# The head of a three-block kernel: first transposes tile by tile, low parts ahead of the next statistics, recursion steps apart

## The reference

```
x = x + 0.5 * ffn(layernorm(x))
x = x + ssm(layernorm(x))
x = x + 0.5 * ffn(layernorm(x))

def ffn(x):                                   # tokens x 256
    shared = silu(x @ sg.T) * (x @ su.T) @ sd.T
    logits = x @ gate_w.T                     # 8 experts
    top_id, score = argmax(logits), sigmoid(max(logits))
    routed = sum over e of swiglu_e(where(top_id == e, x * score, 0))
    return shared + routed

def ssm(x):
    u = conv4(x @ W_in + b_in) + conv_b       # 512 channels, depthwise, causal
    h = tanh(A) h + u * Bp ;  y = Cp . h + Dp * u      # 16 states, step by step
    return silu(y) @ W_out + b_out
```

## Time and profile before

| | us |
|---|---|
| median of 3 executions | 859.96 |
| lowest, highest | 859.24, 860.71 |
| the profiled execution | 860.55 |
| its span in the trace | 858.5 |
| PE busy | 827.7 (96%) |
| DVE, ACT, POOL busy | 485.3, 391.5, 461.1 |

### The profile page before, as it was taken

How to read it: one execution, slowest core, us unless ns; L and a number is a source line. 1 busy time by engine, 2 the same in 40 slices (tenths; PEclk the granted TensorE clock), 3 DMA queues, 4 the chain that set the end, 5 groups by cost and what they waited for, 6 DMA issues and landing times.

```text
span 858.5 us, 16219 instructions
## 1 busy us (share of the span) xinstructions
PE 827.7 (96%) x5302; PEld 720.7 (84%) x5303; DVE 485.3 (57%) x983; ACT 391.5 (46%) x766; POOL 461.1 (54%) x444
## 2 busy tenths in 40 slices
PE   4999999999999999999999999999999999999896
PEld 3678988888888888888888888888888888888786
DVE  7888753333333336678999886867333333333364
ACT  4743323334334434556777787233243434434331
POOL 6528870333333058859999992687330333330584
PEclk9999999999999999998999999999999999999999
DMA  9963553645464337310010015155345564431366
GB/s 309 327 260 105 177 167 118 208 159 215 157 229 163 104 62 144 48 26 13 7 56 26 26 51 197 50 166 192 127 134 198 189 213 174 157 123 43 94 157 179
DMA packets 52005, 119.07 MB, mean 139 GB/s; under 512 B 6442, under 2 KB 39860, under 8 KB 47604
## 3 DMA queue, kind: packets, MB, share of 16 engines
q0 software_dynamic: 16624, 75.25, 27.7%
q1 hardware_dynamic: 34834, 43.15, 15.4%
q10 hardware_dynamic: 498, 0.02, 0.0%
HBM read 83.25 MB, written 35.14 MB: 138 GB/s over the span
## 4 chain that ended last, share of the span: by engine, by line
PE 72%; POOL 14%; DMA 6%; issue 4%; DVE 3%; ACT 1%; POOLq 0%; DVEq 0%; SPq 0%; ACTq 0%
PE bank L424 21%; PE bank L426 21%; PE bank L425 20%; POOL xs_sorted L1868 4%; PE bank L631 4%; POOL yr L2062 3%; PE bank L600 2%; DMA wr_hi<-w_routed 2%; DMA xT_kept<-xTf_odd 2%; POOL acc L1942 2%; POOL wr_lo L1912 2%; DVE v L1554 1%; PE bank L491 1%; POOL wr_lo L1904 1%; PE bank L502 1%
## 5 line engine op out<-in xcount | busy, mean ns | idle before, releaser
L1912 POOL TENSOR_TENSOR wr_lo<-wr_raw,wr_hi 128x3072 fp32r<-128x3072 f32 x14 | 95.5, 6819 | 94.7 <-DMA wr_hi<-w_routed 86.4
L424 PE MATMUL bank<-wr_hi,xT_hi 128*128 x312 | 130.2, 417 | 1.1 <-POOL wr_lo L1912 1.1
L1209 DVE TENSOR_TENSOR hT_lo<-bank,hT_hi 128x512 fp32r<-128x512 f32 x78 | 54.0, 692 | 124.6 <-ACT hT_hi L884 124.6
L1512 DVE TENSOR_TENSOR hf<-sg,bank 128x512 f32<-128x512 f32 x78 | 53.7, 688 | 124.3 <-PE bank L426 124.3
L426 PE MATMUL bank<-wr_lo,xT_hi 128*128 x312 | 123.4, 396 | 0.0
L425 PE MATMUL bank<-wr_hi,xT_lo 128*128 x312 | 122.9, 394 | 0.0
L424 PE MATMUL bank<-xT_hi,ws_hi 128*128 128x512 f32 x256 | 102.5, 400 | 2.2 <-DVE xT_lo L1209 2.2
L425 PE MATMUL bank<-xT_hi,ws_lo 128*128 128x512 f32 x256 | 100.8, 394 | 0.0
L426 PE MATMUL bank<-xT_lo,ws_hi 128*128 128x512 f32 x256 | 100.7, 393 | 0.0
L911 ACT ACTIVATE sg<-bank 128x512 f32<-128x512 f32 x64 | 38.2, 598 | 125.8 <-PE bank L426 115.6
L424 PE MATMUL bank<-wr_hi,hT_hi 128*128 x312 | 93.9, 301 | 1.5 <-DVE hT_lo L1209 1.5
(11 more groups left out here) (249 smaller groups left out, 2182.6 us busy)
## 6 DMA issues: line engine op xcount, KB each, us to landing
wr_raw<-w_routed POOLq DMA_DIRECT2D x16, 1536.0 KB
wr_hi<-w_routed POOLq DMA_DIRECT2D x16, 1536.0 KB
rows<-xs_sorted SPq DMA_DIRECT2D x78, 128.0 KB, 2.4
ys_sorted<-rows SPq DMA_DIRECT2D x78, 128.0 KB
xg<-xT_kept SPq DMA_DIRECT2D x12, 512.0 KB
xT_kept<-xTf SPq DMA_DIRECT2D x9, 512.0 KB, 2.6
acc<-x SPq DMA_DIRECT2D x8, 512.0 KB, 9.8
xs_sorted<-zeros POOLq DMA_DIRECT2D x4, 1024.0 KB, 7.8
```

What stands on the lines that cost most here:

```text
L424: pe.matmul(o, a_hi, b_hi, start=start, stop=False, skip_group_check=True)
L1209: return dve.tensor_tensor(o, full, f32(h), ALU.subtract)
L1512: dve.tensor_tensor(hf[:, 0, :], sg[:, 0, :], MU[:, :], ALU.mult).then_inc(s_mh, 1)
L1912: pool.tensor_tensor(wr_lo[:, e % 2, :], wr_raw[:, :], f32(wr_hi[:, e % 2, :]), ALU.subtract).then_inc(s_wl, 1)
```

## The change

Three things are changed, all in the head.

First, PE no longer waits for all 4 tiles of group 0. DVE raises a new semaphore `s_tile` behind each of the first three tiles of `norm_apply(0)`, and `first_transposes` takes each tile's two transposes behind it. The order changes from bank by bank to tile by tile.

Second, DVE makes `ws_low(0, 0)` and `xt_lo(0)` directly behind `norm_apply(0)`, and `r1_stats(1)` behind these.

Third, the steps `setup_ssm(3)` to `setup_ssm(9)` are put at other places on PE and DVE, each apart from its neighbour, and some of DVE's copies of logits and `s_mult` change places with them.

```
@@ PE
+            def first_transposes():
+
+                for t in range(GT):
+                    if t < GT - 1:
+                        pe.wait_ge(s_tile, t + 1)
+                    else:
+                        pe.wait_ge(s_xn, 1)
+                    for kb in range(KB):
+                        mm = pe.transpose(XT[kb][:, t * P:(t + 1) * P], xg[:, 0, t, kb * P:(kb + 1) * P], ident[:, :])
+                        if t == GT - 1:
+                            mm.then_inc(s_xt, 1)
...
-            r1_transposes(0)
+            first_transposes()
             pe.wait_ge(s_wsl, 1)
             shared_gu(0, 0, 0)
             r1_logits(0)
             setup_ssm(2)
             r1_transposes(1)
+            setup_ssm(3)
             shared_gu(0, 0, 1)
             r1_logits(1)
+            setup_ssm(4)
             r1_transposes(2)
-            setup_ssm(3)
-            setup_ssm(4)
+            setup_ssm(5)
             r1_logits(2)
-            setup_ssm(5)
             r1_transposes(3)
+            setup_ssm(6)
             pe.wait_ge(s_wsl, 2)
             shared_gu(0, 0, 2)
             r1_logits(3)
-            setup_ssm(6)
+            setup_ssm(7)
             r1_transposes(4)
             shared_gu(0, 0, 3)
             r1_logits(4)
+            setup_ssm(8)
             r1_transposes(5)
-            setup_ssm(7)
-            setup_ssm(8)
             r1_logits(5)
+            setup_ssm(9)
             r1_transposes(6)
-            setup_ssm(9)
             setup_ssm(10)
             r1_logits(6)
@@ DVE, norm_apply
+                    if g == 0 and t < GT - 1:
+                        ins.then_inc(s_tile, 1)
                 ins.then_inc(s_xn, 1)
@@ DVE
             norm_apply(0)
-            r1_stats(1)
             ws_low(0, 0)
             xt_lo(0)
+            r1_stats(1)
             r1_stats(2)
             r1_stats(3)
             setup_ssm(1)
...
             r1_copy_logits(0)
             r1_stats(4)
+            setup_ssm(3)
             r1_stats(5)
-            setup_ssm(3)
             r1_copy_logits(1)
             setup_ssm(4)
-            r1_copy_logits(2)
             s_mult(0, 0, 0)
             setup_ssm(5)
+            r1_copy_logits(2)
             r1_stats(6)
+            setup_ssm(6)
             r1_stats(7)
             s_mult(0, 0, 1)
             s_lo(0, 0, 0)
-            setup_ssm(6)
             r1_copy_logits(3)
             norm_apply(6)
+            setup_ssm(7)
             s_lo(0, 0, 1)
             dve.wait_ge(s_hl, 1)
             s_mult(0, 0, 2)
             dve.wait_ge(s_hl, 2)
-            s_mult(0, 0, 3)
-            setup_ssm(7)
             r1_copy_logits(4)
             setup_ssm(8)
+            s_mult(0, 0, 3)
             norm_apply(7)
+            r1_copy_logits(5)
             setup_ssm(9)
-            r1_copy_logits(5)
             ws_low(1, None)
```

More of the change, by code:

```diff
@@ L313, in build @@
         s_fad = sem("gathered_rows_added")
+        s_tile = sem("first_rows_normalized")
         s_out = sem("out_stored")
```

## The result

| | us |
|---|---|
| before, median (5 executions) | 859.96 |
| changed, median (5 executions) | 870.88 |
| lowest, highest | 870.14, 873.29 |
| ratio, 95% interval | 1.0138, 1.0124 to 1.0152 |
| span of the profiled execution, before and changed | 858.5, 867.9 |

What follows compares the result with a forecast made beforehand. Group 7's logits, reached through copies and full-line transfers, were taken to bound the kernel. Zeros 0.5 us later put these logits at 48.1 instead of 47.62: 861.05 us against the profiled execution, median 860.4, range 858.7 to 863.0.

Steps and rivals of the forecast that it cites:

- What bounds the kernel: Head: group 7's logits at 47.62 us set the end, through copies of groups 3, 5, 7 and two 512 KB transfers.
- Part 1: Group 0: PE begins 1.8 us earlier, but ACT's late copy turns this into 0.8 us lost at the logits.
- The clock: PE behind group 0's products: upper level expected to hold, products from 22.6 us on at 0.245 us.
- rival (b): PE's clock, not risen by 17.7, stays low past the gap: up to 3.3 us on PE, 863.6 us; chance 0.20.
- the sum: Whole kernel: group 7's logits at 48.1 instead of 47.62, 0.5 us later, giving a median of 860.4 us.
- The transfers: DMA in the head: zeros down at 43.4 instead of 42.9, group 5's keep landing about 0.5 us later.
- the landing follows the bytes ahead: DMA line: group 5's keep waits for the zeros, so its issue at 41.1 instead of 40.55 matters little.
- Part 2: Recursion steps ahead of transposes: ACT begins group 5's copy at 39.9 at the earliest, 0.5 us later than 39.44.
- The bound on the loss: Slow end of the range: changed kernel at most 863.0 us; chance 0.23 of slower, over 861.7 us.

Runs made afterwards that it cites:

- run 4: Changed kernel with 14 unread products on PE filling the gap between group 0's first products and its logits: 861.78 us, ratio 1.0022.
- run 1: Changed kernel with POOL holding the first expert's weights until group 5's keep has landed: 862.94 us, ratio 1.0040.
- run 14: Kernel before with PE delayed by 6 us and the first expert's weights held until group 5's keep has landed: 863.81 us, ratio 1.0054.
- run 6: Kernel before with only the recursion steps moved to their new places on PE and DVE: 860.96 us, ratio 1.0012.
- run 8: Kernel before with PE delayed by 26 products (6.0 us) ahead of the transposes of group 5: 870.76 us, ratio 1.0122.
- run 13: Kernel before with PE delayed by 6 us and the first expert's weights cut into 4 KB pieces: 867.93 us, ratio 1.0087.
- run 15: Kernel before with PE delayed by 20 products (4.6 us) ahead of the transposes of group 5: 867.91 us, ratio 1.0082.
- run 5: Kernel before with only ws_low(0, 0) and xt_lo(0) moved ahead of group 1's statistics: 862.94 us, ratio 1.0037.

## Why the prediction was wrong

**What bounds the kernel**: right in that the head reaches the end only through the logits of group 7, and these hang on the store of group 5; PE has no gap behind them in either kernel. The store of group 3 had left the path, though: the copy of group 5 was put at 39.9 at the earliest and came at 42.90, waiting for PE.

**Part 1**: the mechanism was right, the sizes a little small. The first product was put at 12.3 and came at 12.77; `norm_apply(1)` at 16.2, it came at 16.61; the logits of group 0 at 20.3, they came at 20.73; the gap at 2.6 us, it was 3.42, the larger for the clock that rose at 16 and had the products done sooner. Nothing behind it gained from the early start, as said.

**The clock**: the first step that failed. The forecast let the clock hold, and its fall stood as rival (b) with a chance of 0.20. It was down behind the gap in the changed kernel and in the low parts alone (logits of group 0: 1.08 us in both). Rival (b) had it another way: the clock not yet risen by 17.7. It rose near 16 and fell in the gap. A gap on PE where before there was none, at the place where the trace before had just shown the rise, deserved more than that. The price of (b), up to 3.3 us on PE, was too high: run 4 gives 2.2 us, since the clock was up again near 26.3, within the second twelve products. That (b) put the store at 44.4 and it came at 44.01 is partly luck: with the clock up (run 4) the transposes of group 5 came at 39.99, 0.6 us later than the 39.4 of the sum.

**The transfers**: the second and larger failure. The zeros were put at 43.4, and POOL went on behind them at 43.08. The sum had group 5's store issued at 41.1 and landing 0.5 us late, the changed kernel issued it at 44.01 and it landed 9.9 us late. Rival (b) said that a store issued behind the weights "lands 3 to 4 us late: 863.6": it passed on the lateness of the issue and kept the 5.81 us of the landing, where 12.22 were measured, and did not use the row that has the meeting in it: the store of group 6, issued at 43.2 before, beside the weights and behind the store of group 5, took 10.3 us to land. Its issue in the trace of the kernel before, with the time to its landing in the last column:

```profile
xT_kept<-xTf SPq DMA_DIRECT2D x1, 512.0 KB, 10.3
```

With these 10.3 us in place of 5.8, and the 1.2 us from the landing to the logits, the sum of (b) would have been 44.4 + 10.3 + 1.2 = 55.9 for the logits of group 7, where 57.48 was measured. Runs 1 and 14, which keep the late issue and take the meeting away, give 8 and 6 us back. I used "the landing follows the bytes ahead" only where it made the delay harmless, the zeros ahead of the store, and not for the 3 MB that would come between.

**Part 2**: right in sign, but not in its path. The steps alone cost 1.0 us where the sum had 0.5, but in run 6 the copy of group 5, put at 39.9, began at 38.86, and the loss was on PE at the lower clock. In the whole change they stand, with part 1, between the 2.4 us by which the store led the weights before and the 0.9 by which it followed them after. How much of that is theirs, no run shows.

**The bound on the loss** was the error of the range: it went up to 863.0, and its slowest case, 863.6, had no price for a change of order between two transfers on different queues, though the trace before had them 2.4 us apart (40.55 and 42.91) and that case crossed this distance.

## What to carry to other kernels

Here the distance between a small transfer on the chain and a large one on another queue was no slack that ends softly: once the small one was issued some 0.8 us behind the large one, it cost a step of 6 us or more. List such pairs on the chain, and see which steps move each of the two. Price a transfer that falls behind such a one from a row in which a like transfer already does. An operation that is made early on one engine at the price of a later one should be followed down the second engine's queue: here one copy behind a waiting `norm_apply` turned 1.3 us gained on PE into 3.4 us idle.

## What the runs showed of the hardware

- A 512 KB store issued 0.8 to 2.6 us behind the start of 3 MB of weights took 11.2 to 12.2 us to land; issued within 0.05 us of it, 4.4 and 5.1; with the weights held back, 4.2 and 2.6; 2.2 us behind, but with the weights in pieces of the store's size, 8.3. Where both queues moved, they moved about as many packets (102 and 101; 178 and 166; with the small pieces 189 and 141), so that the queue with 4 KB packets got a quarter of the bytes beside one with 12 KB packets.
- A store issued while the other queue's transfer ran moved nothing for 2.4 to 4.4 us (behind the zeros before, behind the weights in runs 8, 13 and 15), whatever the pieces.
- PE's clock was up from 16 us on and down at 20.7 us, behind 3.4 us of idle time; with 14 products in that gap it stayed up. It was down behind 2.89 us of idle time in run 5, and near 45.6 us in run 6, where no gap from 34 us on was longer than 1.86 us.
